# Routed experts of a perceiver layer: the transposes of TensorE replaced by block transposes, with the spreading on ScalarE

## The reference, cut to what matters

```python
xt = xn.reshape(B * S, H)                          # 1024 x 512
shared = silu(xt @ Wg_s) * (xt @ Wu_s) @ Wd_s
logits = xt @ W_router + routing_bias              # 7 routed experts
scores, idx = jax.lax.top_k(jax.nn.sigmoid(logits), 2)
scores = scores / jnp.sum(scores, axis=-1, keepdims=True)
wts = jnp.sum(one_hot(idx, 7) * scores[..., None], axis=1)
g = jnp.einsum('th,ehi->tei', xt, Wg_r)            # every matrix 512 x 512
u = jnp.einsum('th,ehi->tei', xt, Wu_r)
combined = jnp.einsum('tei,eih,te->th', silu(g) * u, Wd_r, wts)
```

## Time and profile before

| what | value |
|---|---|
| median of 3 runs | 812.71 us |
| the profiled execution, whole | 809.95 us |
| its span | 808.1 us |
| TensorE busy | 773.6 us (96%) |
| VectorE busy | 517.4 us (64%) |
| ScalarE busy | 355.5 us (44%) |
| GpSimd busy | 301.0 us (37%) |
| granted TensorE clock, mean | 0.994 |

### The profile page before, as it was taken

The page is one execution under the profiler, slowest core; times in us unless marked ns, Lnnn a source line. Parts: engine busy times, 40 slices in busy tenths (PEclk is TensorE's granted clock), DMA queues, the critical chain, the costliest instruction groups (busy, mean ns, idle before and its releaser), DMA issues.

```text
span 808.1 us, 17427 instructions
## 1 busy us (share of the span) xinstructions
PE 773.6 (96%) x6752; PEld 574.0 (71%) x6753; DVE 517.4 (64%) x1125; ACT 355.5 (44%) x913; POOL 301.0 (37%) x157
## 2 busy tenths in 40 slices
PE   4799999999899999989999999899999999999996
PEld 3555455554657778878867877788888888888884
DVE  5799798788652447777788887855364333443335
ACT  4356545661443248852178768523432122211221
POOL 1000000000442833732032213533649999993034
PEclk9999999999899999999999999999999999999999
DMA  9968756683520050040388000030485355531138
GB/s 341 390 252 327 259 218 243 262 326 122 219 105 1 0 149 13 2 138 0 105 312 314 1 0 1 22 137 25 183 306 210 112 206 167 191 135 52 52 114 275
DMA packets 46576, 127.04 MB, mean 157 GB/s; under 512 B 4001, under 2 KB 8353, under 8 KB 40369
## 3 DMA queue, kind: packets, MB, share of 16 engines
q1 hardware_dynamic: 36752, 105.44, 35.9%
q10 hardware_dynamic: 7200, 12.32, 4.4%
q0 software_dynamic: 2560, 8.39, 3.1%
HBM read 101.99 MB, written 24.15 MB: 156 GB/s over the span
## 4 chain that ended last, share of the span: by engine, by line
PE 81%; DVE 5%; DMA 5%; POOL 3%; ACT 3%; issue 2%; SPq 0%; DVEq 0%; ACTq 0%; POOLq 0%
PE scores L611 11%; PE bank L641 11%; PE bank L1137 7%; PE bank L1139 7%; PE bank L1138 7%; DMA nat<-in_ctx_keys 3%; PE bank L691 2%; POOL picked L1379 2%; PE bank L845 2%; PE bank L693 2%; PE bank L851 2%; PE bank L692 2%; PE bank L846 2%; PE bank L626 2%; PE bank L881 2%
## 5 line engine op out<-in xcount | busy, mean ns | idle before, releaser
L1844 DVE STREAM_TRANSPOSE ctxT<-nat 128x1024 f32<-128x1024 f32 (+3 forms) x124 | 116.9, 1004 | 7.8 <-DMA nat<-in_ctx_keys 7.5
L641 PE MATMUL bank<-nat,probT 128*64 128x512 f32 (+1 forms) x416 | 93.9, 597 | 0.1
L1366 POOL TENSOR_TENSOR ring_lo<-ring_raw,ring_hi 128x2048 fp32r<-128x2048 f32 x18 | 83.0, 4611 | 14.5 <-ACT ring_hi L1732 13.3
L1244 POOL TENSOR_TENSOR wq_lo<-wq_raw,wq_hi 128x1024 fp32r<-128x1024 f32 x4 | 9.3, 2352 | 207.6 <-ACT wq_hi L1477 207.6
L1137 PE MATMUL bank<-ring_hi,xg_lo 128*128 x180 | 74.2, 412 | 0.0
L1139 PE MATMUL bank<-ring_hi,xg_hi 128*128 x180 | 70.6, 392 | 0.0
L1138 PE MATMUL bank<-ring_lo,xg_hi 128*128 x180 | 70.1, 389 | 0.0
L2488 DVE TENSOR_TENSOR rhm_lo<-bank,rhm_hi 128x512 fp32r<-128x512 f32 x21 | 14.5, 692 | 80.2 <-ACT rhm_hi L1743 80.2
L641 PEld LDWEIGHTS bank<-nat,probT 128*64 128x64 f32 (+1 forms) x416 | 27.9, 136 | 51.6 <-issue 48.1
L1749 ACT COPY hn<-bank 128x512 f32<-128x512 f32 x22 | 12.9, 588 | 112.0 <-PE bank L1139 112.0
L611 PE MATMUL scores<-ctxT,hn 32*64 32x416 f32 (+8 forms) x1536 | 55.2, 426 | 5.1 <-issue 2.7
(11 more groups left out here) (317 smaller groups left out, 1936.1 us busy)
## 6 DMA issues: line engine op xcount, KB each, us to landing
nat<-in_ctx_keys SPq DMA_DIRECT2D x48, 1024.0 KB, 8.1
ring_raw<-in_Wexp SPq DMA_DIRECT2D x21, 1024.0 KB, 6.3
x_slots<-zeros SPq DMA_DIRECT2D x1, 5632.0 KB, 18.2
y_slots<-zeros SPq DMA_DIRECT2D x1, 5632.0 KB, 32.7
hn<-x_slots ACTq DMA_DIRECT2D x22, 256.0 KB, 4.5
y_slots<-hn ACTq DMA_DIRECT2D x22, 256.0 KB, 3.0
w_raw<-in_Wexp SPq DMA_DIRECT2D x3, 1024.0 KB, 5.3
nat<-in_ctx_keys SPq DMA_DIRECT2D x16, 130.0 KB
```

What stands on the lines that cost most here:

```text
L641: last = nc.tensor.matmul(context_bank(k)[64 * b:64 * b + 64, :], probT[0:n, j, 64 * b:64 * b + 64], nat[k % 2][0:n, b, j, :], start=j == ...
L1366: last = nc.gpsimd.tensor_tensor(ring_lo[at], ring_raw[at], ring_hi.bitcast(F32)[at], ALU.subtract)
L1844: dve.transpose(dst, src).then_inc(columns_ready, 1)
```

## The change

Six things are altered; the matrices and their number are as before.

1. **Rows.** `load_rows` issues four DMAs in place of one. Each brings 128 columns of all the tile's rows, as blocks of 32 rows, to 32 partitions. VectorE then transposes in 32 x 32 blocks (`rows_columns`, now on VectorE) from `hn` into a new SBUF tile `xgT`, and the splitting instructions read `xgT` in place of a PSUM bank. The order of the features that comes out is another one, so the gate and up matrices and the norm's weights (`V_W2B`) are permuted on the host (`by_block`).
2. **Hidden activations.** VectorE transposes `rhm` in 32 x 32 blocks into `rhm_blocks`; ScalarE moves the 16 blocks' rows to their partitions by 16 copies of 32 x 128 into `rhmT` (`hidden_columns_out`); VectorE copies `rhmT` to `rhm_hi` and subtracts for `rhm_lo` (`hidden_split`), both from SBUF. The last tile alone keeps TensorE's transposes.
3. **Who waits for split weights.** The wait for `split_ready` goes from VectorE to TensorE (`routed_hidden`, with the numbers loaded by `needs_of`).
4. **Order.** VectorE now does `routed_mult(t)`, then `rows_columns(t+2)`, then `hidden_split(t)`. ScalarE loads tile `t+3` ahead of Silu of tile `t`, and does the 16 copies of tile `t` ahead of `output_rows(t-1)`.
5. **Entrance.** The third matrix of the second expert is loaded first (`order_of`), not held back by the scatter; ScalarE rounds it ahead of the row loads, and GpSimd splits it as soon as its scatters are issued. VectorE's third `ring_lo` instruction goes behind the first two tiles' rows.
6. **Router.** Each matmul of `router` becomes four of 32 tokens.

The core of the diff:

```diff
-                for m in range(3):
+                for m in order_of(e):          # (2, 0, 1) for e == 1
+                    if e == 1 and m == 0:
+                        sp.wait_ge(scattered, 16 * 2 * NT)
...
             def router(k):
                 for c in range(HC):
-                    last = nc.tensor.matmul(bank[3][:, NE * k:NE * k + NR], xf[k % 4][:, c, :], wrout_sb[:, c, :],
-                                            start=c == 0, stop=c == HC - 1)
+                    for m in range(P // B32):
+                        own = slice(B32 * m, B32 * (m + 1))
+                        last = nc.tensor.matmul(bank[3][own, NE * k:NE * k + NR], xf[k % 4][:, c, own], wrout_sb[:, c, :],
+                                                start=c == 0, stop=c == HC - 1, skip_group_check=True)
...
-            def routed_hidden(t, par, at, turn=None):
-                if not (isinstance(t, int) and t < 2):
-                    hidden_columns(t - 1)
+            def routed_hidden(t, par, at, need=None):
                 pe.wait_ge(xgT_ready, t + 1)
+                if need is not None:
+                    pe.wait_ge(split_ready, need)
                 for m, b, full in ((gate, 1, rgate_full), (up, 2, rup_full)):
...
-                    if m == gate and turn is not None:
-                        rows_columns(t + 1, 1 - par, turn)
...
-            pool.wait_ge(scattered, 16 * 2 * NT)
-            pool.wait_ge(slots_ready, 5)
-            pool.wait_ge(split_ready, 1)
             for e in range(1, NR):
-                for m in range(3):
+                for n, m in enumerate(order_of(e)):
...
+                    if e == 1 and n == 2:
+                        pool.wait_ge(split_ready, 1)
                     last = nc.gpsimd.tensor_tensor(ring_lo[at], ring_raw[at], ring_hi.bitcast(F32)[at], ALU.subtract)
...
             def load_rows(t, par):
-                nc.scalar.dma_start(xg[par][:], x_slots[ds(t * P, P), :]).then_inc(xg_loaded[par], 16)
+                for c in range(HC):
+                    nc.scalar.dma_start(xg[par][B32 * c:B32 * (c + 1)], slot_rows(t)[c]).then_inc(xg_loaded[par], 16)
...
             def hidden_columns_out(t):
-                act.wait_ge(rhmT_full, t + 1)
-                nc.scalar.copy(hidden_parts(t)[0][:].rearrange("p c q -> p (c q)"), bank[3][:]).then_inc(rhm_split, 1)
+                act.wait_ge(rhm_turned, 2 * t + 1)
...
+                    for g in range(4):
+                        for a in range(4):
+                            last = nc.scalar.copy(rhmT[B32 * a:B32 * (a + 1), :, B32 * g:B32 * (g + 1)],
+                                                  rhm_blocks[B32 * g:B32 * (g + 1), :, a, :])
...
             def routed_step(t, par, turn, load=True):
                 if load:
-                    act.wait_ge(xgT_full, t + 1)
-                    load_rows(t + 2, par)
+                    act.wait_ge(xgT_full, t + 2)
+                    load_rows(t + 3, 1 - par)
                 routed_silu(t)
...
+                hidden_columns_out(t)
+                output_rows(t - 1, 1 - par, turn)
...
+            def rows_columns(t, par, turn):
+                dve.wait_ge(xg_loaded[par], 64 * turn)
...
+                dve.transpose(xgT[:].rearrange("p a (g q) -> p a g q", q=B32),
+                              xg[par].rearrange("p g (a e) -> p a g e", e=B32)).then_inc(xgT_full, 1)
                 dve.wait_ge(xgT_full, t + 1)
                 for c in range(HC):
-                    last = dve.tensor_scalar(xg_hi[par][:, c, :], columns[c], weights[c], None, ALU.mult)
+                    last = dve.tensor_scalar(xg_hi[par][:, c, :], xgT[:, c, :], vec[:, V_W2B + c:V_W2B + c + 1], None, ALU.mult)
...
+                dve.tensor_copy(rhm_hi[:], rhmT[:]).then_inc(rhm_turned, 1)
+                dve.wait_ge(rhm_turned, 2 * t + 2)
+                dve.tensor_tensor(rhm_lo[:], rhmT[:], rhm_hi.bitcast(F32)[:], ALU.subtract).then_inc(rhmT_ready, 1)
...
+            def hidden_and_next(t, par, turn):
+                routed_mult(t)
+                rows_columns(t + 2, par, turn + 1)
+                hidden_split(t)
```

More of the change, by code:

```diff
@@ L300, in perceiver_kernel @@
         rhm = place(172, "rhm", [P, D])
+        rhm_blocks = place(156, "rhm_blocks", [P, HC, 4, B32])
+        rhmT = place(158, "rhmT", [P, HC, P])
         rhm_hi = place(174, "rhm_hi", [P, HC, P], F32R)
@@ L2467, in rows_columns_out @@
                 dve.wait_ge(xgT_full, t + 1)
-                columns = [bank[6 + par][:, c * P:(c + 1) * P] for c in range(HC)]
-                weights = [vec[:, V_W2 + c:V_W2 + c + 1] for c in range(HC)]
                 for c in range(HC):
-                    last = dve.tensor_scalar(xg_hi[par][:, c, :], columns[c], weights[c], None, ALU.mult)
+                    last = dve.tensor_scalar(xg_hi[par][:, c, :], xgT[:, c, :], vec[:, V_W2B + c:V_W2B + c + 1], None, ALU.mult)
                 last.then_inc(xg_split, 1)
@@ L2473, in rows_columns_out @@
                 dve.wait_ge(xg_split, t + 1)
-                dve.wait_ge(split_ready, nth)
                 for c in range(HC):
-                    last = dve.scalar_tensor_tensor(xg_lo[par][:, c, :], columns[c], weights[c], xg_hi[par].bitcast(F32)[:, c, :],
-                                                    ALU.mult, ALU.subtract)
+                    last = dve.scalar_tensor_tensor(xg_lo[par][:, c, :], xgT[:, c, :], vec[:, V_W2B + c:V_W2B + c + 1],
+                                                    xg_hi[par].bitcast(F32)[:, c, :], ALU.mult, ALU.subtract)
@@ L2483, in routed_mult @@
                 dve.tensor_tensor(rhm[:], rhm[:], bank[2][:], ALU.mult).then_inc(rhm_ready, 1)
+                if not (isinstance(t, int) and t == TILES - 1):
+                    dve.wait_ge(rhm_ready, t + 1)
+                    dve.transpose(rhm_blocks[:].rearrange("p c a q -> p (c a q)"), rhm[:]).then_inc(rhm_turned, 1)
             def hidden_split(t):
                 dve.wait_ge(rhm_split, t + 1)
-                hi, lo = hidden_parts(t)
-                dve.tensor_tensor(lo[:].rearrange("p c q -> p (c q)"), bank[3][:],
-                                  hi.bitcast(F32)[:].rearrange("p c q -> p (c q)"), ALU.subtract).then_inc(rhmT_ready, 1)
@@ L2491, in _ @@
-            rows_columns_out(0, 0)
-            down_out(NT - 1)
-            rows_columns_out(1, 1)
-            routed_mult(0)
-            hidden_split(0)
-            with dve.Fori(0, TILES // 2 - 1) as i:
+                if isinstance(t, int) and t == TILES - 1:
+                    hi, lo = rhm_last
+                    dve.tensor_tensor(lo[:].rearrange("p c q -> p (c q)"), bank[3][:],
+                                      hi.bitcast(F32)[:].rearrange("p c q -> p (c q)"), ALU.subtract).then_inc(rhmT_ready, 1)
+                    return
@@ new lines, in hidden_split @@
+                if not (isinstance(t, int) and t == 0):
+                    dve.wait_ge(rdown_full, t)
+                dve.tensor_copy(rhm_hi[:], rhmT[:]).then_inc(rhm_turned, 1)
+                dve.wait_ge(rhm_turned, 2 * t + 2)
+                dve.tensor_tensor(rhm_lo[:], rhmT[:], rhm_hi.bitcast(F32)[:], ALU.subtract).then_inc(rhmT_ready, 1)
+            for k in range(NT - 2):
+                down_out(k)
+                if k in (3, 4):
+                    first_low(k - 3)
+            rows_columns(0, 0, 1)
@@ L2499, in _ @@
[L2499 to L2501 removed]
+                    hidden_and_next(2 * i + 2 + par, par, i + 2)
+            routed_mult(TILES - 2)
+            hidden_split(TILES - 2)
             routed_mult(TILES - 1)
```

116 lines of the change are left out of this document (55 added, 61 removed).

## The result

Median 894.3 us (890.1 to 897.3) beside 812.6 (811.2 to 813.4); ratio 1.100, 95% interval 1.096 to 1.105. Forecast were 911 and the range 855 to 932. The profiled execution has a span of 891.6 us beside 808.1: 83.5 more, and the multiplications say where. In order: tiles 0, 1, 2 and 18 on VectorE (timeline: start us, us, instruction; they answer to the earlier trace rows; M(t) is the start of tile t's multiplication from here on).

The account below looks back on a forecast made before the run. TensorE was taken to set the pace, 9.11 us a tile. The terms 31.4 + 11.7 + 56 + 2.7 - 4 = +98 on the profiled 809.95 gave 908, and 911 as median, 2.8 above; range 855 to 932.

Parts of the forecast that it names:

- Turns between VectorE and GpSimd: VectorE's ten SBUF-only instructions per tile: during a split one passes per GpSimd instruction, of 4.11 us on average.
- Rival 1: GpSimd is let in only between groups, four scalings passing as one turn: +67, 880 us; chance 0.20.
- rival 2: No collision at 128 columns, only ScalarE's longer chain of steps per tile: +14, 827 us; chance 0.10.
- Entrance: Entrance and first splits: VectorE held by GpSimd, tile 2's multiplication at 649.1 instead of 617.66, +31.4 us.
- first gate product at 601.1: At the entrance: GpSimd holds the scalings until 598.8, then 2.3 us for the eight instructions.
- Rival 4: TensorE idles some 10 us in each split and its clock may fall to 1.2 GHz: 930 and over; chance 0.04.
- ScalarE's ring: Silu, multiplication, transpose, copies, store and loads in sequence: 9.84 us a tile against 9.11, +11.7 over 16 tiles.
- Tile 2 to 18: Sixteen tiles: +11.7 us from ScalarE's steps per tile and +56 from four experts' splits.
- Then six GpSimd instructions [...] with six turns of VectorE between them: One expert's split, fourth to seventh: 24.7 us plus about 2.0 of turns; delay +14.1 each, +56 for four.
- Copy of tile 18 and what follows: At the end: this copy now stands behind tile 19's 16 copies, 14.6 us after tile 18's multiplication, not 11.9: +2.7.
- Signs named beforehand: In the profile: long VectorE instructions, splits beyond 780 us, TensorE below 80% awaiting rhm_lo, copies 4.9 us, 9.8 between multiplications.
- the rival of a faster kernel: No collision and overlapping ScalarE copies of 0.20 us each, 8.1 us of steps per tile: -13, 800 us; chance 0.06.

Follow-up runs that it names:

- the first experiment: The changed kernel with xgT and rhmT in PSUM banks 6 and 7 instead of SBUF: 831.9 us, ratio 1.025 to the kernel before.
- GpSimd's pieces: The changed kernel with each split instruction of GpSimd cut into four of 128 x 512: 877.0 us, ratio 1.080 to the kernel before.
- the written-out loop: TensorE's loop over tile pairs written out, values loaded between gate and up: 807.0 us on the PSUM kernel with later loads and rows first; 880.2 on the changed kernel.
- the half change: Row blocks transposed by VectorE into PSUM, rhm by TensorE as before, router in four, first rows ahead of weights: 807.8 us, 0.995 of the kernel before.
- rows-first variant: PSUM kernel with loads behind Silu, plus second expert's first two matrices sent only after the first tile's rows land: 828.9 us, 1.021 of the kernel before.

## Why the prediction was right, and where its steps were off

- *Turns between VectorE and GpSimd* (the large term): right, mechanism and place. Taken away, with 0.56 us a tile of shorter copies, it gives 62 of the 82 us back. Rival 1 (a group passes as one turn) fell with the 12.25 us for four `xg_lo`; rival 2's 827 is the first experiment.
- *Entrance*, +31.4 forecast, 27.4 with the router's -4 that falls ahead of it; +29.7 measured. The step "first gate product at 601.1" came at 601.19, but partly by luck: the rows landed only at 596.2, 1.7 us after VectorE was ready for them, which the step doesn't have. Then M(0) was 2.8 later than forecast; TensorE had idled 5.2, and from 601 to 606 its granted clock was 0.50, the level of 1.2 GHz. Rival 4's mechanism was there. From 598 to 872 us the clock was 0.50 for 72 us in all, and TensorE was busy for 43 of them; so it cost at most 22 us (an estimate, half of the 43), some of which ScalarE's ring hides. How much of it reached the time isn't separated.
- *Tile 2 to 18*, +67.7 forecast (11.7 ring, 56 splits), +49.1 measured. Here terms were mis-sized against each other. The ring is 10.3, not 9.84 (a gap of 0.2 ahead of the loads, 0.08 more for their issue, and 0.24 of handovers where 0.1 was taken): 16 x (10.3 - 9.11) = 19. That leaves 30 where 56 was forecast, and 14 of the 30 go away with the loop head, which the prediction has not at all. The other 16 are the late splits: 4 each, not 14.1. The step that failed is "Then six GpSimd instructions [...] with six turns of VectorE between them": a split comes in two parts, since the third matrix is fetched only after the down product. Of the 58.3 us that GpSimd waited for loads, 37.5 (four waits) stand ahead of a split's first matrix and 20.7 (four waits, 1.8 to 11.2) ahead of its third. VectorE caught up meanwhile: in the wait shown, between 742 and 753 us, its scalings took 0.29 us each again.

```profile
POOL ring_hi L1362 <- DMA ring_raw<-in_Wexp: 58.3, 8, 17.1
...
753.18 3.60 POOL L1362 TENSOR_TENSOR ring_hi<-ring_raw,cst 128x2048 fp32r<-128x2048 f32 x1 [11.17 <-DMA ring_raw<-in_Wexp]
```
- *Copies on ScalarE*: 4.94 forecast, 4.90 measured. The Trainium skill's overlap ("ScalarE: Activation LUTs", "What ACT_TABLE_LOAD costs") isn't seen in this trace either: one copy takes 0.296 us, and they start 0.307 apart.
- *Copy of tile 18 and what follows*: +2.7 forecast, +4.7 measured from M(18) to the end. *Router*: -4 forecast, -1.9 alone (0.5 to 3.2).
- *Signs named beforehand*: GpSimd's splits went on beyond 780 us, the 16 copies took 4.9 and TensorE waited for `rhm_lo`, as forecast. But TensorE was 88% busy, not below 80%, and of the four means only that of `rhm_lo` passed 1 us (1.49; `xg_hi` 0.88, `rhm_hi` 0.72, `xg_lo` 0.61).
- *Chances*: the rival of a faster kernel wasn't absurd. Without the collision and the loop head, the same idea gives 0.99, with the tiles 8.2 apart that this rival named. What it asked of the copies (under 0.21 each) wasn't needed: they took 0.26 there, with the loads issued where ScalarE waits for VectorE.

So 911 against 894 is a sum of a too large term (-40 on the splits), of two that were too small or missing (+7, +14), and of three of 2 each (ahead of M(2), behind M(18), and the median's distance from the profiled execution, which was less). The mechanism was right; that the number came this near was in part luck, since the splits' term was over three times too large.

Not tried: other sizes of GpSimd's pieces together with the written-out loop, and the loop head with an empty queue behind it measured by itself. Whether the 5.41 us go by value or by load instruction is open; three fewer values took about 2 us or more off. The time of the lower clock wasn't varied by itself either.

## What to carry to other kernels

Before an operation is moved off TensorE, look where its replacement reads and writes: here the same instructions cost some 60 us with their source in SBUF beside a busy GpSimd, and with it in PSUM they kept their times. A time that meets the expectation doesn't confirm the bound behind it; take that bound away next. And a releaser named by the profile is the last event, not the cause: compare the distance to each candidate over several rounds. The constant one is the candidate to take away in the next experiment.

## What the runs showed of the hardware that was not expected

- TensorE's loop head with six register values: gate product 5.41 us after the last semaphore before it, round after round. It was hidden in the half change, where the next instruction isn't due until 6.0 us after that semaphore; with three values no gap was left at 3.5 us.
- After an idle time of 1.8 us at that head TensorE's granted clock was 0.64 from 704 to 708 us. Such a tile was 3.7 us longer than one of 8.2. In two rounds of the rows-first variant (gate products at 645.1 and 723.8 us) it idled 1.9 us, the clock stayed at 1.00, and the tile was only 2.1 longer; so about 2.1 are the idle time and 1.6 the clock.
- Sixteen 32 x 128 copies by ScalarE: 4.90 us from SBUF to SBUF, 4.34 from SBUF to PSUM.
- Row loads of 64 KB beside the weights' 3 MB took up to 7.9 us to land (first PSUM variant). With the second and third of those weights held back until the first tile's rows had landed, the entrance's median was 2.0 (loads between 586 and 600 us, variant with the rows first; the columns are KB each and the median to landing):
```profile
DMA to landing us min/median/max: 1.8/1.9/7.9
```
```profile
hn<-x_slots ACTq DMA_DIRECT2D x9, 64.0 KB, 2.0
```
